# Two layers of attention on one core: the score matmuls by halves of two heads, the bias last on GpSimd, and two VectorE steps in other slots

## What is computed

```
xn  = layernorm(x)
# linear attention, causal
q, k, v = elu(xn @ wq) + 1, elu(xn @ wk) + 1, xn @ wv
S_t = S_(t-1) + k_t v_t^T ;  z_t = z_(t-1) + k_t
o_t = (q_t S_t) / (q_t . z_t + eps)
# softmax attention
q, k, v = xn @ Wq.T + bq, xn @ Wk.T + bk, xn @ Wv.T + bv
attn = softmax(((q / |q|) + query_embedding) * softplus(temperature) @ k^T / sqrt(32))
h    = attn @ v
gain = (from a softmax over 15 routed and 2 shared gates of h)
out  = x + o @ wo + (h * gain) @ Wp.T + bp
```

## Time and profile before

| | us |
|---|---|
| median of 3 executions | 4141.6 (4140.52 to 4141.78) |
| the profiled execution | 4145.29 |
| its span in the trace | 4143.4 |
| PE busy | 3907.7 (94%) |
| DVE busy | 3387.2 (82%) |
| ACT busy | 2809.0 (68%) |
| POOL busy | 346.6 (8%) |

### The profile page before, as it was taken

One profiled execution on the slowest core, in us unless ns is written; L12 is line 12 of the kernel. 1 busy time (PEld: TensorE's weight loads), 2 busy tenths in 40 slices (PEclk: granted clock), 3 DMA queues, 4 the chain that ended last, 5 costly groups with the idle time before them and its releaser, 6 DMA issues.

```text
span 4143.4 us, 87939 instructions
## 1 busy us (share of the span) xinstructions
PE 3907.7 (94%) x36031; PEld 1603.2 (39%) x36032; DVE 3387.2 (82%) x3532; ACT 2809.0 (68%) x3833; POOL 346.6 (8%) x229
## 2 busy tenths in 40 slices
PE   3889999999999999999999999999999999999999
PEld 1533433333333434433433434434433333433323
DVE  5668888888887888888798888888788788788887
ACT  2457777777777677667667677676677677676663
POOL 3100000000000000000000000000000000000120
PEclk8889999999999999999999999999999999999999
DMA  5322212222222213223222222223222222222223
GB/s 211 102 63 57 70 51 58 58 68 56 55 74 83 83 56 98 71 63 92 75 71 77 82 66 85 82 65 87 59 61 78 69 65 63 83 63 61 67 84 111
DMA packets 366538, 313.07 MB, mean 76 GB/s; under 512 B 159448, under 2 KB 314552, under 8 KB 365492
## 3 DMA queue, kind: packets, MB, share of 16 engines
q1 hardware_dynamic: 365412, 298.98, 24.9%
q10 hardware_dynamic: 720, 8.39, 0.5%
HBM read 231.26 MB, written 76.01 MB: 74 GB/s over the span
## 4 chain that ended last, share of the span: by engine, by line
issue 62%; PE 23%; POOL 5%; ACT 4%; DVE 4%; DMA 1%; SPq 1%; ACTq 0%; POOLq 0%; DVEq 0%
PE ps L1225 5%; PE ps L1211 5%; PE ps L1084 5%; ACT prob L908 3%; POOL rn L731 3%; PE ps L1181 3%; DVE acc L1756 2%; PE ps L1092 1%; POOL y L704 1%; PE ps L1129 1%; PE ps L1109 1%; SPq L429 1%; PE ps L1155 1%; PE ps L1121 0%; PE ps L1137 0%
## 5 line engine op out<-in xcount | busy, mean ns | idle before, releaser
L908 ACT ACTIVATE prob<-ps 128x1024 f32<-128x1024 f32 x2048 | 1985.1, 1022 | 530.3 <-PE ps L1211 497.7
L1756 DVE TENSOR_TENSOR acc<-acc,prob 128x2048 f32<-128x2048 f32 x896 | 2053.4, 2292 | 32.2 <-ACT prob L908 15.6
L1225 PE MATMUL ps<-prob,v 128*32 128x512 f32 x8192 | 1091.2, 605 | 0.0
L1211 PE MATMUL ps<-q_hi,k_hi 32*128 32x512 f16 x4096 | 422.7, 385 | 124.2 <-ACT prob L908 122.3
L1211 PE MATMUL ps<-q_lo,k_hi 32*128 32x512 f16 x4096 | 411.9, 374 | 0.0
L1211 PE MATMUL ps<-q_hi,k_lo 32*128 32x512 f16 x4096 | 411.9, 374 | 0.0
L1084 PE MATMUL ps<-x_hi,w_hi 128*128 128x512 f16 x1024 | 395.9, 387 | 3.0 <-ACT rdl L856 2.3
L1084 PE MATMUL ps<-x_lo,w_hi 128*128 128x512 f16 x1024 | 393.9, 385 | 0.0
L1084 PE MATMUL ps<-x_hi,w_lo 128*128 128x512 f16 x1024 | 392.8, 384 | 0.0
L1181 PE MATMUL ps<-wop_hi,fin 128*128 128x512 f16 x1024 | 331.2, 382 | 4.2 <-DMA y<-in_x 2.5
L1225 PEld LDWEIGHTS ps<-prob,v 128*32 128x32 f32 x8192 | 161.3, 108 | 433.4 <-issue 433.4
(11 more groups left out here) (261 smaller groups left out, 4443.5 us busy)
## 6 DMA issues: line engine op xcount, KB each, us to landing
x_hi<-xhi_scratch SPq DMA_DIRECT2D x64, 512.0 KB, 6.7
x_lo<-xlo_scratch SPq DMA_DIRECT2D x64, 512.0 KB, 8.0
x_in<-in_x SPq DMA_DIRECT2D x64, 256.0 KB, 7.4
rq<-rq_scratch SPq DMA_DIRECT2D x64, 256.0 KB
rdl<-rdl_scratch SPq DMA_DIRECT2D x64, 256.0 KB
y<-in_x SPq DMA_DIRECT2D x64, 256.0 KB, 6.1
out<-y SPq DMA_DIRECT2D x64, 256.0 KB, 6.0
rden<-rden_scratch SPq DMA_DIRECT2D x63, 256.0 KB
```

The lines of the kernel that those rows point to most:

```text
L908: s_.activation(prob[i % 3][:, 2 * p:2 * p + 2, :], ps[:, 2 * p:2 * p + 2, :], ACT.Exp, bias=-SHIFT, scale=1.0 / CQK).then_inc(exped, 1)
L1211: last = t_.matmul(bank[h], kk[rows32(h), cols128(kt)], qq[rows32(h), :], start=(kk is kh and qq is qh), stop=(kk is kl and not wide))
L1225: last = t_.matmul(bank[OUT][rows32(h), :], v[m // NB % 2][:, kt, rows32(h)], prob[i % 3][:, h, :], start=(kt == 0), stop=(kt == TT - 1))
L1756: v_.tensor_tensor(acc[:], acc[:], prob[i % 3][:], ALU.add).then_inc(summed, 1)
```

## The change

POOL does the bias after its two powers. The four state additions of a block move on DVE from slot 14 of the step that prepares the block to slot 1 of the next step. The division of the linear output moves on DVE from slot 6 to slot 5. The scores are issued as two halves of two heads, each with its own wait for the exponentials of the same two heads of the slot before and its own increment, and ACT waits for each half apart.

```
             for s in range(FIRST, LAST + 1):
                 n, t = prepared(s), norm_tile(s)
-                if out_tile(s) is not None:
-                    add_bias(out_tile(s))
                 if t is not None:
                     rstd_of(t)
                 if n is not None:
                     pool.wait_ge(ss_kept, n + 1)
                     pool.wait_ge(rns_done, n)
                     g_.tensor_tensor(rn[:], ss[:], minus_half[:], ALU.pow).then_inc(rn_done, 1)
+                if out_tile(s) is not None:
+                    add_bias(out_tile(s))
...
-                act.wait_ge(scored, i + 1)
                 for p in range(2):
+                    act.wait_ge(scored, 2 * i + p + 1)
...
             def score(m, kt, wide):
                 i = m * TT + kt
-                pe.wait_ge(exped, 2 * i)
                 kh, kl = k_hi[m // NB % 2], k_lo[m // NB % 2]
                 qh, ql = q_hi[m % NRING], q_lo[m % NRING]
-                for kk, qq in ((kh, qh), (kh, ql), (kl, qh)):
-                    for h in range(HG):
-                        last = t_.matmul(bank[h], kk[rows32(h), cols128(kt)], qq[rows32(h), :], start=(kk is kh and qq is qh),
-                                         stop=(kk is kl and not wide))
...
-                last.then_inc(scored, 1)
+                for half in range(2):
+                    if i:
+                        pe.wait_ge(exped, 2 * (i - 1) + half + 1)
+                    heads = (2 * half, 2 * half + 1)
+                    for kk, qq in ((kh, qh), (kh, ql), (kl, qh)):
+                        for h in heads:
+                            last = t_.matmul(bank[h], kk[rows32(h), cols128(kt)], qq[rows32(h), :], start=(kk is kh and qq is qh),
+                                             stop=(kk is kl and not wide))
...
+                    last.then_inc(scored, 1)
...
+                    if kt == 1 and p is not None:
+                        states(p)
...
-                        if p is not None:
-                            divide_o(p)
...
                         mask(n, 0)
-                        states(n)
...
+                    if kt == 5 and p is not None:
+                        divide_o(p)
```

More of the change, by code:

```diff
@@ L1205, in score @@
                 i = m * TT + kt
-                pe.wait_ge(exped, 2 * i)
                 kh, kl = k_hi[m // NB % 2], k_lo[m // NB % 2]
                 qh, ql = q_hi[m % NRING], q_lo[m % NRING]
-                for kk, qq in ((kh, qh), (kh, ql), (kl, qh)):
-                    for h in range(HG):
-                        last = t_.matmul(bank[h], kk[rows32(h), cols128(kt)], qq[rows32(h), :], start=(kk is kh and qq is qh),
-                                         stop=(kk is kl and not wide))
[L1213 to L1216, removed]
-                last.then_inc(scored, 1)
+                for half in range(2):
[6 more added lines that the diff above has]
+                                             stop=(kk is kl and not wide))
+                    if wide:
+                        for h in heads:
+                            last = t_.matmul(bank[h], mone[rows32(h), :], mrow[rows32(h), m % NB * QN:(m % NB + 1) * QN], start=False,
+                                             stop=True)
+                    last.then_inc(scored, 1)
             def weigh(m, kt):
```

## The result

The changed kernel takes 4120.64 us (median of 5, 4117.63 to 4124.38) against 4141.6 us for the kernel before (median of 5, run beside it). The ratio is 0.9949 [0.9937, 0.9962]: 21.0 us less. The forecast was 4126.0, 15.4 less, with a range from 4112 to 4155. Run once more beside two other kernels, the changed kernel gave 4122.64 against 4143.96, ratio 0.9944 [0.9931, 0.9958].

What follows compares the result with a forecast made beforehand. PE, busy 94%, was taken to set the pace in 799 of 1024 score groups, with delays from POOL's late power. Terms 8.0 - 19.8 - 3.6 = -15.4 us took 4141.6 to 4126 us, range 4112 to 4155.

Steps and rivals of the forecast that it cites:

- The POOL order (-19.8): Steps 16 to 59: with the bias last, POOL's powers no longer wait for late `y`; -19.8 us.
- the delay is hidden anyway: Rival: slot 8 scores often waited for something else, so only a third of 19.8 comes; 4139 us, chance 0.08.
- The division before the main loop (-3.6): Steps -3 to -1: dividing earlier on DVE shortens the path 1.2 us each; -3.6 us, bounds 0 and -4.1.
- The price of the halves (+8.0): Scores on PE: half 1 starts 0.01 us late in 799 unwaited groups; 8 us, near bounds 0 and 16.
- The gain of the halves (0): Waited score slots on PE: half 1 still needs the second exponentials; gain 0, upper bound 122.3 us.
- a total wait near 120 us: Sign of being right: PE's total wait for exponentials stays near 120 us, now on half 1.
- the halves remove the waits too: Rival on PE's score waits: at most 122.3 us more gained, half if handed on, 4065 us; chance 0.07.
- Strict order (the rival at 4470): Rival: score matmuls never overtake, half 1 starts two rounds late, +352 us, 4470 us; chance 0.08.
- The 26.3 ns for an increment: Skill's cost per semaphore increment behind concurrent tiles; the scores' second increment would cost up to 21 us, unseen in rows.
- The states (0): DVE's four state additions, slot 14 to slot 1: cost 0, at most 81 us if their cover is gone.
- The sum: Whole kernel: 8.0 - 19.8 - 3.6 = -15.4 us, giving 4126 us from 4141.6.
- as the prediction said they would: Sign of being right: steps 16 to 59 repeat with 61.2 us each.

Runs made afterwards that it cites:

- fill_gaps: Changed kernel with, in steps 0 to 15, key-value products in slot 12 instead of 13 and the denominators' matmul in slot 14 instead of 15: 4091.54 us, ratio 0.9869.
- head_major: Changed kernel with each head's three score matmuls issued one behind the other: 4128.96 us, ratio 0.9957.
- cols_halves: Changed kernel with every score matmul cut in two of 256 columns, still by halves, for timing alone: 4280.91 us, ratio 1.0326.

## Why the prediction was right, step by step

**The POOL order (-19.8): right, in place and size.** Alone it gives -19.9 us, all of it in steps 16 to 59. In the changed kernel these steps are 18.5 us shorter, because the halves cost 1.5 us there. What was priced was the whole chain in the earlier trace rows, and every link of it went with the first one. The rival that the delay is hidden anyway is refuted.

**The division before the main loop (-3.6): right, a little less.** In steps -3 to -1 the time from xt_lo to the norms' multiplication (qb), the stretch that holds the division, ACT's copy, the stores and the spread of the norms, was read from the timelines of all kernels. First the kernel before, DVE, steps -3 and -1, then the changed one:

```profile
152.14 0.67 DVE L1545 TENSOR_TENSOR xt_lo<-ps,xt_hi 128x512 f16<-128x512 f32 x1
...
161.80 0.69 DVE L1664 TENSOR_TENSOR qb<-qb,rq 128x512 f32<-128x512 f32 x1 [1.37 <-DMA rq<-rq_scratch]
...
228.48 0.67 DVE L1545 TENSOR_TENSOR xt_lo<-ps,xt_hi 128x512 f16<-128x512 f32 x1
...
241.57 0.69 DVE L1664 TENSOR_TENSOR qb<-qb,rq 128x512 f32<-128x512 f32 x1 [3.01 <-DMA rq<-rq_scratch]
```

```profile
155.53 0.67 DVE L1549 TENSOR_TENSOR xt_lo<-ps,xt_hi 128x512 f16<-128x512 f32 x1
...
164.31 0.69 DVE L1668 TENSOR_TENSOR qb<-qb,rq 128x512 f32<-128x512 f32 x1 [0.48 <-DMA rq<-rq_scratch]
...
228.20 0.67 DVE L1549 TENSOR_TENSOR xt_lo<-ps,xt_hi 128x512 f16<-128x512 f32 x1
...
240.25 0.69 DVE L1668 TENSOR_TENSOR qb<-qb,rq 128x512 f32<-128x512 f32 x1 [1.98 <-DMA rq<-rq_scratch]
```

It falls from 9.66 to 8.78 and from 13.09 to 12.05 us, and in step -2 from 9.90 to 8.88. The three together are 32.6 to 33.3 us in the four kernels that divide in slot 6 and 29.2 to 30.1 us in the nine profiles that divide in slot 5; the means, 32.9 and 29.6, differ by 3.3 us. The bounds were 0 and 4.1. One pair of profiles can't show it: the first scores of step 0 start 1.5 us earlier here, but between 242.5 and 252.0 us in the nine profiles and between 251.5 and 253.9 in the four. On the mean they come 5.1 us earlier (247.6 against 252.8), so that before step 0 the division gives 3.3 us in the stretch that was priced and perhaps more in all. The spread is too wide to say: xt_lo of step -3 alone starts between 151.1 and 155.9 us in the nine profiles, 3.39 us later here than in the kernel before. Why was not settled.

**The price of the halves (+8.0): the step that was mis-sized.** It was reckoned as 799 unwaited groups x 0.01 us. Each of them does pay about that: unwaited slots go from 3.26 to 3.27, 3.16 to 3.17, 4.45 to 4.46 and 3.72 to 3.73 us in steps 50 and after. The term left out what waited groups give back. Slots 1 and 2 together go from 8.52 to 8.50 us, slots 5 and 6 from 7.43 to 7.41. The rows of step 50 show where from: ACT waits only for the scores of two heads, and starts its exponentials 0.94 us after the first score instead of 0.96, and half 1 is issued while half 0 runs, so that the weighing follows its start after 0.75 us instead of 0.76. In steps 52 to 55 the balance is 244.94 - 244.80 = 0.14 us in four steps, so 44 / 4 x 0.14 = 1.5 us in steps 16 to 59. Steps 60 to 63 cost nothing more. In steps 1 to 15 the halves even gain 1.2 us: most of these steps take 57.91 us instead of 58.01, in the changed kernel and with the halves alone, and the 0.10 us come from slots 11 to 15. Together that is 1.5 - 1.2 = **0.3 us**, where 8 had been taken; the halves alone measured -1.6, from -5.4 to +2.1. The mechanism (half 1 is held only by its instructions' issue) was right: 0.02 us between the halves' loads, weighing after 0.77 us.

**The gain of the halves (0): right but for steps 1 to 15.** There several waited slots follow one another, the case in which the forecast allowed a gain, and it thought that ACT's start would not be early; the 1.2 us say that a little came. That this is the reason is argued, not tried. Elsewhere PE's wait is still there, within the group. The forecast's sign for this, a total wait near 120 us, did not appear as such. That the named wait fell to 6.7 us looks like the rival "the halves remove the waits too"; fill_gaps, which took 33 us out of just these waits, shows that it is not.

**Strict order (the rival at 4470): refuted** by the halves alone and by head_major. The sentence of the Trainium skill, "TensorE: Matmul & The Clock Gate", section "The mechanism", that matmuls start strictly in program order, doesn't hold among row groups in these runs: heads 2 and 3 started at 2037.31, ahead of matmuls before them in the program at 2037.41. Even in cols_halves half 1 starts with three matmuls for each row group of half 0 still to come. The 26.3 ns for an increment of the section "The cost: per-tile semaphore tail" did not appear: an unwaited slot is 0.01 us longer (3.27 for 3.26), and that is the whole price of the second half, its wait and its increment.

**The states (0): right**, ratio 0.9999.

**The sum** was -15.4. With the sizes as measured it is -19.9 - 3.3 + 0.3 = -22.9, and -21.0 was measured, with an interval from -26.1 to -15.7. Of the difference, 0.7 us is in step 0 of the changed kernel (58.38 us instead of 57.68), which no term held. The halves were overpriced by 7.7 us and the forecast is only 5.6 us short of the measured gain; that is luck, and the interval is wider than either. Steps 16 to 59 repeat with 61.01, 61.01, 61.64 and 61.27 us, 61.2 on the mean, as the prediction said they would.

## What to carry to other kernels

An engine that is idle nine tenths of the time can hold up all others by the order of its few instructions: put what waits for a late transfer behind what others wait for, and price it by whole steps, disturbed against undisturbed (19.8 us forecast, 19.9 measured). A wait split over two halves of a group disappears from the list of waits and turns into busy time; look at the time between the halves before you believe it. When PE waits in one slot and is overfull in the next, as it still is here, moving a few matmuls forward is worth more (63 us, measured on top of the halves) than making the wait finer (-1.6 us, not told from nothing).

## What the runs showed of the hardware

Matmuls on a free row group start ahead of earlier ones in the program that are queued for a busy one: with each head's three matmuls in a row, the first ones of four heads still start together (2008.61 in `head_major`). The freedom has a limit. With two busy row groups, two or three matmuls queued behind the running one of each let the next ones through (3265.05 in the changed kernel); with five the next ones were held until three were left, 0.24 us in the group shown, and the kernel took 149 us more.

A busy share of 97% says little of an array that is filled by row groups: a half that runs alone counts as much as a full group. In `cols_halves` it was 98%, with the longest time of all kernels here.
